# First six periods of a cross-attention and expert kernel put in another order, with a second way to LN2's scale for two batches

## What is computed

```python
q, k, v = proj_split(layernorm(x), W_Q), proj_split(ctx, W_K), proj_split(ctx, W_V)
scores = einsum('bhqd,bhkd->bhqk', q, k) / sqrt(16)
attn = softmax(scores, axis=1)                      # over the eight heads
x = x + einsum('bsd,ed->bse', merge(einsum('bhqk,bhkd->bhqd', attn, v)), W_O)
t = layernorm(x)
logits = t @ Wr + br                                # top 2 of 8, softmax of these two
h = relu(einsum('btd,edh->bteh', t, W1) + b1)       # hidden size 256
x = x + einsum('bte,bteh,ehd->btd', gates, h, W2) + gates @ b2
```

## Time and profile before

| | us |
|---|---|
| median of 3 timed runs (lowest, highest) | 210.2 (209.53, 210.39) |
| the profiled execution, its own time | 210.6 |
| its span in the profile | 208.7 |
| PE busy (share of the span) | 198.9 (95%) |
| DVE (VectorE) busy | 167.7 (80%) |
| ACT (ScalarE) busy | 132.5 (63%) |
| POOL (GpSimd) busy | 112.0 (54%) |

### The profile page before, as it was taken

The page is one execution under the profiler, slowest core; times in us unless marked ns, Lnnn a source line. Parts: engine busy times, 40 slices in busy tenths (PEclk is TensorE's granted clock), DMA queues, the critical chain, the costliest instruction groups (busy, mean ns, idle before and its releaser), DMA issues.

```text
span 208.7 us, 4954 instructions
## 1 busy us (share of the span) xinstructions
PE 198.9 (95%) x1736; PEld 176.0 (84%) x1736; DVE 167.7 (80%) x453; ACT 132.5 (63%) x316; POOL 112.0 (54%) x132
## 2 busy tenths in 40 slices
PE   6999878698999999999999999999999999999995
PEld 6846776587799979997999899998998899789994
DVE  6498779779789999899888988898999897556533
ACT  2236847678577847787677767587757776445441
POOL 8503657849976387719662856466846674010000
PEclk9999999889999999999999999999999999999999
DMA  5659576806506153314041504241001000000000
GB/s 177 156 135 296 155 236 176 239 25 177 153 21 180 33 152 102 105 52 124 12 149 47 176 3 135 71 133 45 3 0 28 0 2 0 28 0 5 25 3 25
DMA packets 20264, 18.70 MB, mean 90 GB/s; under 512 B 1776, under 2 KB 18704, under 8 KB 20240
## 3 DMA queue, kind: packets, MB, share of 16 engines
q1 hardware_dynamic: 17344, 16.85, 27.6%
q10 hardware_dynamic: 2896, 1.54, 2.7%
HBM read 11.83 MB, written 6.55 MB: 88 GB/s over the span
## 4 chain that ended last, share of the span: by engine, by line
PE 91%; DVE 3%; ACT 2%; issue 1%; POOL 1%; POOLq 0%; DVEq 0%; ACTq 0%
PE y_ps L431 28%; PE h_ps L416 22%; PE score_ps L356 7%; PE misc_ps L375 6%; PE score_ps L344 6%; PE h_ps L364 4%; PE score_ps L277 3%; PE misc_ps L396 2%; PE score_ps L333 2%; PE score_ps L416 2%; PE misc_ps L384 2%; PE misc_ps L282 1%; PE misc_ps L322 1%; PE misc_ps L301 1%; PE misc_ps L295 1%
## 5 line engine op out<-in xcount | busy, mean ns | idle before, releaser
L688 ACT ACTIVATE hT<-h_ps,b_sb 128x256 f32<-128x256 f32 x118 | 49.5, 471 | 34.1 <-PE h_ps L416 32.9
L431 PE MATMUL y_ps<-w_sb,hT 128*128 128x128 f32 x508 | 68.0, 277 | 0.0
L431 PEld LDWEIGHTS y_ps<-w_sb,hT 128*128 128x128 f32 x508 | 62.8, 191 | 3.4 <-issue 2.2
L1181 POOL TENSOR_TENSOR half_sum<-e_sb 128x512 f32<-128x512 f32 x28 | 37.2, 1330 | 32.0 <-ACT e_sb L660 31.6
L931 DVE TENSOR_TENSOR attn<-e_sb,e_rcp 128x1024 f32<-128x1024 f32 x32 | 42.2, 1320 | 3.3 <-ACT e_rcp L671 3.3
L923 DVE TENSOR_REDUCE shift_m<-score_ps 128x128 fp32r<-128x1024 f32 x32 | 38.8, 1214 | 3.5 <-PE score_ps L344 2.3
L416 PE MATMUL h_ps<-x1T_hi,w_lo 128*128 128x256 f32 x118 | 38.1, 322 | 1.3 <-ACT hT L688 0.6
L660 ACT ACTIVATE e_sb<-score_ps 128x1024 f32<-128x1024 f32 x32 | 32.8, 1025 | 5.6 <-PE score_ps L356 5.4
L1000 DVE SCALAR_TENSOR_TENSOR acc<-y_ps,gates,acc 128x128 f32<-128x128 f32 x96 | 29.1, 344 | 8.6 <-PE y_ps L431 7.3
L416 PE MATMUL h_ps<-x1T_hi,w_hi 128*128 128x256 f32 x118 | 33.4, 283 | 0.0
L416 PE MATMUL h_ps<-x1T_lo,w_hi 128*128 128x256 f32 x118 | 33.3, 283 | 0.0
(11 more groups left out here) (115 smaller groups left out, 285.5 us busy)
## 6 DMA issues: line engine op xcount, KB each, us to landing
k_scratch<-k_parts SPq DMA_DIRECT2D x14, 256.0 KB, 2.6
k_stack<-k_scratch SPq DMA_DIRECT2D x14, 256.0 KB, 3.9
q_stack<-q_scratch SPq DMA_DIRECT2D x28, 128.0 KB, 2.7
q_scratch<-q_parts SPq DMA_DIRECT2D x7, 256.0 KB, 2.1
w_sb<-in_w SPq DMA_DIRECT2D x1, 1024.0 KB, 6.8
out_y<-y_out SPq DMA_DIRECT2D x7, 128.0 KB, 1.9
x_all<-in_x ACTq DMA_DIRECT2D x1, 768.0 KB, 6.5
ctxT<-in_ctx_t SPq DMA_DIRECT2D x1, 640.0 KB, 5.2
```

Source lines behind the costliest of these rows:

```text
L431: mm = nc.tensor.matmul(product(j, t), hT[:, j % 2, c, t * P:(t + 1) * P], w2_sb[:, e * HC + c, :], start=(c == 0), stop=(c == HC - 1))
L688: op = nc.scalar.activation(hT[:, j % 2, c, :], hidden(j)[:, c * S:(c + 1) * S], ACT.Relu, bias=b1_sb[:, e * HC + c:e * HC + c + 1])
L1181: nc.gpsimd.tensor_tensor(half_sum[:], e[:, 0:HQ // 2], e[:, HQ // 2:HQ], ALU.add).then_inc(sum_step, 1)
```

## The change

It touches the lists of `beginning()` on all five engines, five helpers, and nothing in `period(i)`.

- SyncE: w1's transfer comes first of all (bound to the arrival of x and the context of batch 1), and for batches 1 and 2 both spills stand ahead of both stack loads.
- LN2 of batches 0 and 1 (`QUICK = 2`): ScalarE takes the logarithm of the variance and the Exp of -0.5 times it (`quick_rstd`), and VectorE makes x1n in two `tensor_scalar` (`quick_x1n`). GpSimd's `ln2_end` and ScalarE's `make_x1n` are left for batches 2 to 7.
- PE: dummies of 4 and 2 in place of 5, 1 and 2, and two new places, 5 ahead of `scores(2, 0)` and 4 ahead of `expert_up(0, 0)`, in `y_ps`.
- LN1 is taken batch by batch (eight calls in place of five), those of batches 6 and 7 near the end of `beginning()`.
- GpSimd's memset of `q_stack[:, 1]` moves from ahead of the first power to behind the second.
- The other new names (`FIRST = 1`, the tuple `PE_SUMS`, an index in `k_first` and `q_wide`) leave the same values as before.

SyncE, and the dummies' new form:

```diff
 x_rows = x.rearrange("b (t p) d -> p (b t) d", p=P)
 sp.dma_start(x_all[:, 0:TT, :], x_rows[:, 0:TT, :]).then_inc(x0_in, 16)
 sp.dma_start(ctxT[:, 0, :], ctx_t[0]).then_inc(ctx_in[0], 16)
+sp.wait_ge(x1_in, 16)
+sp.wait_ge(ctx_in[1], 16)
+sp.dma_start(w1_sb[:], w1.rearrange("e d h -> d e h")).then_inc(w1_in, 16)
 spill_k(1)
-sp.dma_start(w1_sb[:], w1.rearrange("e d h -> d e h")).then_inc(w1_in, 16)
+spill_q(1)
 load_k_stack(1)
-spill_q(1)
 load_q_stack(1)
+sp.dma_start(ctxT[:, 3:B, :], ctx_t[3:B].rearrange("b d s -> d b s")).then_inc(ctx_rest_in, 16)
 spill_k(2)
-sp.dma_start(ctxT[:, 3:B, :], ctx_t[3:B].rearrange("b d s -> d b s")).then_inc(ctx_rest_in, 16)
+spill_q(2)
 load_k_stack(2)
-spill_q(2)
 load_q_stack(2)
 ...
-def keep_warm(n):
-    for _ in range(n):
-        nc.tensor.matmul(score_ps[:, 1, 0:P], ident[:], ident[:], start=True, stop=True, skip_group_check=True)
+def keep_warm(times, dst, freed, n):
+    wait(pe, freed, n)
+    for _ in range(times):
+        nc.tensor.matmul(dst, ident[:], ident[:], start=True, stop=True, skip_group_check=True)
```

PE, `beginning()` as far as the second expert:

```diff
 def beginning():
     project_k(0, None, 0)
+    keep_warm(4, score_ps[:, 1, 0:P], None, 0)
+    transpose_xn(0, None, 0)
+    keep_warm(2, score_ps[:, 1, 0:P], None, 0)
+    project_q(0, xnT_taken, 1)
     project_v(0, None, 0)
-    keep_warm(5)
-    transpose_xn(0, None, 0)
-    keep_warm(1)
-    project_q(0, xnT_taken, 1)
     project_k(1, k_first_made, 1)
-    keep_warm(2)
-    first_scores(0)
-    project_k(2, None, 0)
-    first_scores(1)
+    first_scores(0, 0)
+    first_scores(0, 1)
     transpose_xn(1, q_wide_made, 2)
     subtract_max(0, 0)
+    project_k(2, None, 0)
     project_q(1, xnT_taken, 2)
     subtract_max(0, 1)
-    first_scores(2)
+    first_scores(0, 2)
     head_sum(0, 0, k_lo_made, 1)
-    first_scores(3)
+    first_scores(0, 3)
     subtract_max(0, 2)
     transpose_xn(2, k_lo_made, 2)
     head_sum(0, 1, log_made, 1)
+    subtract_max(0, 3)
     project_q(2, xnT_taken, 3)
-    subtract_max(0, 3)
     head_sum(0, 2, log_made, 2)
     scores(1, 0)
     head_sum(0, 3, log_made, 3)
-    project_v(1, v_taken, 1)
+    subtract_max(1, 0)
     scores(1, 1)
-    subtract_max(1, 0)
+    scores(1, 2)
     attend_values(0, q_lo_made, 2)
     subtract_max(1, 1)
     project_out(0, heads_taken, 1)
-    project_v(2, x1_made, 1)
-    scores(1, 2)
+    project_v(1, v_taken, 1)
+    subtract_max(1, 2)
     scores(1, 3)
-    transpose_x1n(0, v_taken, 3)
-    subtract_max(1, 2)
+    project_k(3, x1_made, 1)
+    keep_warm(5, y_ps[:, 0, 0:P], q_lo_made, 1)
+    scores(2, 0)
+    subtract_max(1, 3)
+    transpose_xn(3, k_lo_made, 3)
+    transpose_x1n(0, xnT_taken, 4)
+    keep_warm(4, y_ps[:, 0, 0:P], q_lo_made, 1)
     expert_up(0, 0)
-    scores(2, 0)
-    route(0, x1T_lo_made, 1)
+    project_q(3, x1T_lo_made, 1)
+    subtract_max(2, 0)
+    scores(2, 1)
+    route(0, q_lo_made, 3)
+    expert_down(0, 0)
+    scores(2, 2)
     expert_up(0, 1)
-    subtract_max(1, 3)
-    project_k(3, logits_made, 1)
-    expert_down(0, 0)
```

ScalarE, the new function and the list's first half:

```diff
+def quick_rstd(b):
+    act.wait_ge(ln2_var_made, b + 1)
+    nc.scalar.activation(ln2_log[:], ln2_var[:], ACT.Ln).then_inc(ln2_log_made, 1)
+    act.wait_ge(ln2_log_made, b + 1)
+    nc.scalar.activation(ln2_rstd[:], ln2_log[:], ACT.Exp, scale=-0.5).then_inc(ln2_quick_made, 1)
 ...
+    exponentiate(1, 0)
     split_w1(3)
-    make_xn(3)
-    split_w1(4)
-    exponentiate(1, 0)
-    split_w1(5)
-    take_v(1)
-    split_w1(6)
     take_heads(0)
     exponentiate(1, 1)
     invert_sum(1, 0)
+    quick_rstd(0)
+    exponentiate(1, 2)
+    take_k_hi(3)
+    split_w1(4)
+    take_xnT(3)
+    invert_sum(1, 1)
+    take_x1T_hi(0)
+    exponentiate(1, 3)
+    take_q_hi(3)
+    relu(0, 0)
+    exponentiate(2, 0)
```

VectorE, the new function and the list as far as the first gated addition:

```diff
     nc.vector.tensor_scalar(ln2_var[:], ln2_mv[:, :, 1], EPS, None, ALU.add).then_inc(ln2_var_made, 1)
-    nc.vector.tensor_scalar(ln2_neg[:], ln2_mv[:, :, 0], -1.0, None, ALU.mult).then_inc(ln2_neg_made, 1)
+    if b >= QUICK:
+        nc.vector.tensor_scalar(ln2_neg[:], ln2_mv[:, :, 0], -1.0, None, ALU.mult).then_inc(ln2_neg_made, 1)
+
+def quick_x1n(b):
+    dve.wait_ge(ln2_quick_made, b + 1)
+    wait(dve, x1T_done, b)
+    for t in range(TT):
+        op = nc.vector.tensor_scalar(x1n[:, t, :], x1[:, t, :], ln2_mv[:, t, 0:1], ln2_rstd[:, t:t + 1],
+                                     ALU.subtract, ALU.mult)
 ...
 def beginning():
     dve.wait_ge(x1_in, 16)
-    ln1(TT, 2 * TT, 1)
-    spread_q(0)
-    ln1_end(1, 1)
-    k_lo(1)
-    spread_q(1)
+    ln1(1)
+    spread_q(0, 0)
+    ln1_end(1)
+    spread_q(0, 1)
     head_max(0, 0)
     head_max(0, 1)
+    k_lo(1)
     dve.wait_ge(x_in, 16)
-    ln1(2 * TT, 3 * TT, 2)
+    ln1(2)
+    q_lo(1)
+    ln1(3)
+    head_max(0, 2)
     k_lo(2)
-    q_lo(1)
-    head_max(0, 2)
-    ln1(3 * TT, 5 * TT, 3)
+    ln1(4)
     head_max(0, 3)
+    split_wr()
     normalize(0, 0)
+    q_lo(2)
     normalize(0, 1)
-    split_wr()
-    q_lo(2)
+    head_max(1, 0)
     normalize(0, 2)
-    head_max(1, 0)
     normalize(0, 3)
     head_max(1, 1)
-    ln1(5 * TT, NT, 4)
+    head_max(1, 2)
+    ln1(5)
     add_residual(0)
     ln2(0)
-    head_max(1, 2)
     head_max(1, 3)
+    normalize(1, 0)
+    k_lo(3)
+    quick_x1n(0)
+    head_max(2, 0)
     x1T_low(0)
-    normalize(1, 0)
-    head_max(2, 0)
+    normalize(1, 1)
+    q_lo(3)
+    head_max(2, 1)
     take_logits(0)
     choose_experts(0)
-    normalize(1, 1)
-    k_lo(3)
-    head_max(2, 1)
+    normalize(1, 2)
+    head_max(2, 2)
+    normalize(1, 3)
     make_gates(0)
     transpose_gates(0)
-    normalize(1, 2)
-    normalize(1, 3)
-    q_lo(3)
+    head_max(2, 3)
     add_expert(0, 0)
```

GpSimd:

```diff
-    ln1_rstd_of(TT, 2 * TT, 1)
+    ln1_rstd_of(1)
+    nc.gpsimd.memset(q_stack[:, 1].bitcast(F32), 0.0).then_inc(q_zeroed[1], 1)
+    ln1_rest(2)
+    ln1_rest(3)
     nc.gpsimd.memset(q_stack[:, 0].bitcast(F32), 0.0).then_inc(q_zeroed[0], 1)
-    ln1_rest(2 * TT, 3 * TT, 2)
     split_w1(0)
-    ln1_rest(3 * TT, 5 * TT, 3)
+    ln1_rest(4)
     split_w1(1)
+    head_sum(1, 0)
     split_w1(2)
     split_w1(3)
-    split_w1(4)
-    head_sum(1, 0)
-    ln2_end(0)
     head_sum(1, 1)
     head_sum(1, 2)
+    split_w1(4)
     head_sum(1, 3)
-    ln1_rest(5 * TT, NT, 4)
+    head_sum(2, 0)
     split_w1(5)
-    head_sum(2, 0)
+    head_sum(2, 1)
     split_w1(6)
-    head_sum(2, 1)
-    ln2_end(1)
+    head_sum(2, 2)
     split_w1(7)
-    head_sum(2, 2)
     head_sum(2, 3)
+    ln1_rest(5)
     head_sum(3, 0)
     head_sum(3, 1)
+    ln1_rest(6)
     ln2_end(2)
     head_sum(3, 2)
     head_sum(3, 3)
+    ln1_rest(7)
```

314 lines of the change are left out of this document (158 added, 156 removed).

## The result

The changed kernel takes 214.0 us (median of four runs, 213.5 to 215.7) against 210.0 for the kernel before (209.5 to 210.4): 1.020 times as long, 95% interval 1.016 to 1.025. The forecast was 207.7 with a range to 210.9. The profiled execution took 213.47 us with a span of 211.7, against 210.6 and 208.7. Executions more than 1.5% above the fastest of their kernel count as slow, and the medians and ratios of all runs here leave them out.

What follows compares the result with a forecast made beforehand. The prediction took PE as the bound, waiting in the opening and full afterwards. Its terms, +0.3 − 1.0 − 1.3 − 0.5 = −2.5 us, took the profiled 210.6 to 208.1, so a median of 207.7 us, range 205.2 to 210.9.

Steps and rivals of the forecast that it cites:

- Residual of batch 0 at 32.7: Batch 0's residual sum on VectorE, at 34.34 us before, comes 1.7 us earlier; bounds 1.2 and 2.3.
- w1 against x, none taken: w1's transfer beside the remaining x in the opening: no delay counted, worst cost 1.8 us.
- First up +0.3: First expert up-projection on PE: at 39.6 us, against 39.24 before, 6.6 us after the residual plus contention.
- its sign of being wrong: The prediction called itself wrong if the first up-projection moved by more than 1.5 us either way.
- The contention term: VectorE's two x1n instructions beside GpSimd: 0.3 us lost, out of a possible 0 to 2.2.
- Moved ahead of the first up −1.0: Scores and a maximum subtraction moved into PE's idle time before the first up-projection: 1.0 us gained.
- clock dip −1.3: PE's drop to half clock in the microsecond from 40 us is gone: 1.3 us gained, bounds 0 and 1.7.
- Waits after the first up −0.5: PE's other waits between first up-projection and hand-over: 1.6 of 2.1 us stay, 0.5 us gained.
- The VectorE ledger: VectorE's busy time from 51.70 to 85.63 us: −0.2 us work, arriving 1.4 earlier with idle unchanged, 5.1 with none.
- Same period behind it, hand-over's shift equal to the total's: After the opening's six periods: still 22.1 us per period, hand-over's shift within 0.5 us of the total's.
- The slower rival: x1n of batch 0 comes 4 us late on VectorE, delaying expert work: +1.6 us, 211.8 us, chance 0.13.
- The second rival: VectorE's idle stays 3.7 us and the lock costs 1 us: −0.4 us, 209.8 us, chance 0.15.

Runs made afterwards that it cites:

- e7: The changed kernel with GpSimd held back from its sum over batch 1's second pair until VectorE has made x1n of batch 0; 213.76 us.
- e2: The changed kernel without its two late dummy places (five and four dummies on PE); 216.02 us.
- e9: The changed kernel with most of GpSimd's sums over exponentials left out for batches 1 to 3; 209.26 us.
- e5: The changed kernel with K and Q of batch 3 and V of batch 2 moved behind the first expert, x1n directly behind a maximum; 214.16 us.
- e6: The changed kernel with the first gated addition put ahead of the maximum over batch 2's fourth pair on VectorE; 214.11 us.
- e1: The changed kernel with LN2 of batches 0 and 1 made the old way (GpSimd's power, ScalarE's normalizing); 211.51 us.
- e11: The changed kernel with the old LN2 for batches 0 and 1 and most of GpSimd's sums left out for batches 1 to 3; 208.57 us.

## Why the prediction was wrong

It was wrong in sign, and mainly on one assumption: that VectorE's instructions keep their usual length beside GpSimd. By its own steps:

- *Residual of batch 0 at 32.7:* 33.30. The scores of batch 1 still waited, for 1.57 us at 25.27. The spill was out early (15.11 for 16.78) but the load, issued at 18.52, took SyncE 3.0 us to issue in place of 1.76. Off by 0.6.
- *w1 against x, none taken:* right. The large x landed 6.1 us after its issue at 2.74 (6.5), with w1 issued at 5.33 beside it, and VectorE took batch 2's moments at 13.59 without a wait.
- *First up +0.3:* **+1.8, the first step that failed.** It is also past the 1.5 us that the prediction named as its sign of being wrong. The residual gives 0.6. The contention term was 0.3 and measured 1.16 (1.76 − 0.60), one stall of the two that its upper bound of 2.2 allows. The rest of the walk was right: 7.71 − 1.16 = 6.55 us from the residual, for 6.6 (though the pieces it lists add up to 6.25). The reason for the 0.3, "most instructions of VectorE beside GpSimd show their usual length", read the wrong instructions: maxima and additions out of PSUM do. So does the BN_STATS at 33.76 (0.49 us beside a half sum), which reads one tensor in SBUF. Products and the x1n pair don't. The Trainium skill (SBUF — State Buffer, Who interferes with whom), which the prediction had beside it, says that a VectorE instruction in a two-port mode, `tensor_scalar` named, and a GpSimd instruction lock each other out. The trace agrees for this pair: 1.76 us beside a half sum, 0.60 in e7 with GpSimd idle.
- *Moved ahead of the first up −1.0, clock dip −1.3:* both happened on PE in the profiled execution, which worked 3.8 us in place of 2.8 from 34 to 39, at clock 1.00. The hand-over was late even so, for VectorE took more than they gave; that the clock counts is plain from e2, 2.0 us slower without the dummies. The 1.3 was also a little large, and could not all reach the median: executions of the kernel before without the dip are 0.4 to 1.1 us faster, and 36 of 60 had none to begin with.
- *Waits after the first up −0.5:* **the step that failed most.** From first up to hand-over the prediction had −2.8 us for all its terms; measured is +1.15 (44.74 for 43.59). The VectorE ledger was the right tool and held wrong lengths. It gave the run "an x1n pair (+0.6)" and left the products at their old length. Measured were 1.97 us for the pair and 1.43 for a product, with VectorE's idle time falling from 5.9 to 3.8 us in the stretch. With GpSimd's sums cut, e9 goes from the first up to the hand-over in 40.7 us, where the forecast's terms give 40.8: the rest of the ledger stood.
- The products: the Trainium skill's same section says more than the prediction took from it: a `tensor_tensor` with both inputs in SBUF contends with a GpSimd instruction that reads SBUF, in no two-port mode at all. The trace agrees: the product reads two SBUF tiles and took 2.27 us beside a half sum, 1.23 otherwise. The same section says that a `tensor_reduce` never contends, and the trace agrees there as well: the maximum stays at 1.21 us throughout (it reads PSUM here, so this tests little).
- *Same period behind it, hand-over's shift equal to the total's:* right (22.11 us; 2.9 and 3.0).

The slower rival, 211.8 us with a chance of 0.13, named the place and the lock, and wanted "both lock stalls, 2.2", for batch 0's pair: that pair lost 1.16 us. What no rival held are batch 1's pair (1.37) and the products (1.0 us on the one at 48.95, 0.6 on one at 67.78, less on others). The gates' small operations are no part of the loss: they take 4.7 us in the stretch before and after. The second rival ("VectorE gives it back") had the right engine and priced the lock at 1 us; over the stretch the stalls that the kernel before doesn't have are 4.3 us, and e9's cut takes 5.6 off VectorE (48.67 − 43.10), 1.7 of it from the gates' operations.

Why the products of the kernel before stood so little while GpSimd was busy just as long (35.09 us against 35.10) isn't settled. The collisions are not absent there: its gates' operations are stretched as much, and its half sums take 1.42 us on average where 1.28 is usual. But the three additions of a unit take 2.62 us there on average and 3.10 in the change. Before, GpSimd waits for exponentials (2.8 us ahead of its half sum at 45.77), and products fall in such gaps; e5 and e7 show that moving one instruction moves the collision to another. What rule would place them all well wasn't tried.

## What to carry to other kernels

Before giving an engine a new instruction, ask from where it reads. In these traces the VectorE instructions that took turns with GpSimd are those with two inputs in SBUF and the `tensor_scalar` from SBUF; price such a one by the worst row at once if VectorE has little idle time. And in e5, e6 and e7 a wait of PE that was closed by reordering came back a few steps later, with VectorE busy for 90 to 93% of the stretch; count its busy time over the whole stretch, stalls included, before looking at any one path.

## What the runs showed beyond expectation

- A stalled instruction counts as busy. VectorE's busy time rose by 6.1 us in the stretch, with almost nothing listed as idle before these groups (0.0 us); only the mean of a group (1426 for 1231 ns) gives the stall away.
- GpSimd stands as well as VectorE. In e7, a quarter sum that began 0.6 us behind a product took 1.59 us for 0.73:

```profile
42.02 1.60 DVE L959 TENSOR_TENSOR attn<-e_sb,e_rcp 128x1024 f32<-128x1024 f32 x1 [1.16 <-ACT e_rcp L688]
...
42.62 1.59 POOL L1218 TENSOR_TENSOR quarter_sum<-half_sum 128x256 f32<-128x256 f32 x1
```

- Small operations suffer most in proportion. The one that writes batch 0's gates took 1.19 us in the change:

```profile
53.11 1.19 DVE L1003 TENSOR_TENSOR gates<-gated_onehot 128x16 f32<-128x16 f32 x1
```

  It took 0.18 us before. But one row misleads: the `gap_exp` of batch 1 took 1.27 us before and 0.16 in the change, and over both batches the gates' operations (twelve) take 4.73 us before and 4.67 after.

- The first transposes of xn came between 7.1 and 8.4 us in profiles of kernels whose starts are the same (the change, e1, e2, e5 to e7, e9, e11). A profile is one execution, and a microsecond of its span can be that; lengths between two marks in it are safer to compare.
